# Four running tables in place of eight in a graph network's scatter, zeros written at the start, and a new order of two attention loops

## The chip, the cores and the metric

The kernel runs on one core of one Trainium2 chip. The metric is device time in microseconds (us), lower is better. Before the change three runs gave a median of 5661.89 us (5657.54 to 5664.57).

## What is computed

A graph with 3125 nodes of 128 features (padded to 3200, that is 25 blocks of 128) and 103125 edges, sorted by destination, goes through four layers: a GCN, an additive attention with 4 heads, a GAT with 2 heads, and an interaction layer. Each adds its result to `x`. The change touches the last one most. Cut to that, the reference is:

```python
xa = ssp(x)                          # softplus(x) - log 2
g = rbf @ k2f_W                      # one filter row per edge, from 64 attributes
msg = g * (xa @ Wj + bj)[idx_j]      # idx_j is the edge's destination
xj = segment_sum(msg, idx_i, n)      # idx_i is its source: in no order
m = xa @ Wi + bi + xj                # then residual blocks and a dense layer
```

The attention layers (additive and GAT) do for each edge: gather the source's projected row, add the destination's, apply tanh or leaky ReLU, multiply by an attention vector to a score, take a softmax over the edges of a destination, and sum the weighted source rows by destination.

## The kernel before, in words

Edges are cut into 202 tiles of 512 (`TILE`), four chunks of 128 (`SUB`). The kernel is a row of stages. A stage opens a block in which each engine has a program of its own, held together by semaphores; at its end all engines meet at a barrier (class `Stage`). SP issues the plain DMAs, POOL the indirect ones.

**`over_tiles`** (line 73) writes out the software pipeline of one engine: in step s it calls each function of its list, in the order of the list, for tile s minus that function's lag. The order of the list is thus the order in which an in-order engine does its work in a step. The change edits three such lists in `attend` (line 1321):
- on PE, for GAT, line 1461: scores (1412, 1415), turn_sums (1457), features (1399, 1403), sums (1443), turn (1424), turn_top (1434);
- on ACT, for the additive layer, line 1501: raise_scores (exp, line 1482), activate (tanh, 1476), keep_sums (1494);
- on DVE, for GAT, line 1552: tops (1521 to 1528), keep_sums (1548), onehots (1158), leaky (1514), edge_weights (1535), best_of_nodes (1541, 1544).

In both layers POOL gathers 128 rows for each chunk (line 744); a tile's gathers wait until the sums of the tile six before are done.

**`count_degrees`** (line 769), near the start, counts destinations: DVE makes one-hots (line 790) in 101 steps and PE multiplies them. SP has nothing to do until the counts are inverted; then it stores them (842) and loads them back (845, 847).

**The interaction.** `load_sources` (line 2079) loads the edges' sources, and clears eight tables in DRAM of 3200 + 128 rows of 128 float32: DVE makes 3200 zeros in each partition (2091), SP stores them eight times (2102), and 128 spare rows eight times (2104). The stage ends when all stores have landed. Then `scatter_filtered` (line 1162) makes 512 messages for each tile on PE, ACT and DVE: DVE compares the sources of a chunk with each other (1268), masks what lies above the diagonal (1273), so that a row that occurs twice in a chunk is summed by PE (1235) and goes out once, and the other is sent to a spare row (1295). ACT copies the rows out (1251). Last, POOL sends each chunk with an indirect DMA that adds into a table in DRAM (1309). Such a DMA reads its rows, adds, and writes them back, so two of them on the same table must not be under way at once. Table `sums[i][j]` is that of the tiles of parity i and chunk j, and so a chunk's scatter waits for that of the tile two before:

```python
for j in range(SUB):
    wait_count(pool, scattered[t.two][j], half_rounds(t) * 16)
pool.sem_inc(begun, 1)
for j in range(SUB):
    pool.indirect_dma_start(out=k.sums[t.two][j], ...)
```

ACT (1250) and DVE (1294) wait for the scatters of the tile four before, whose buffers they write over. `collect_sums` (line 2109) loads the eight tables one after another in three buffers (2122), and DVE copies the first (2132) and adds the other seven (2134).

Of the kernel before, what the change touches and what calls it, by code (L numbers as in the profile page):

```python
# [33 lines left out]
P = 128  # L34
# [134 lines left out]
def load_everything(k):  # L169
# [95 lines left out]

    k.sums = [[nc.dram_tensor(f"sums{i}_{j}", [N + P, F], F32).ap() for j in range(SUB)] for i in range(2)]
    k.all_counts = nc.dram_tensor("counts", [T, P, k.cells], FP16).ap()
# [501 lines left out]
def count_degrees(k):  # L769
# [23 lines left out]
    with Stage(k, "deg") as st:  # L793
        step, digits, high_ready, low_ready, counted = (st.sem("step"), st.sem("digits"), st.sem("high_ready"),
                                                        st.sem("low_ready"), st.sem("counted"))
        rooted, inverted, stored, spread = st.sem("rooted"), st.sem("inverted"), st.sem("stored"), st.sem("spread")
        with st.block() as block:
            @block.vector
            def _(dve):
# [39 lines left out]
            @block.sync  # L839
            def _(sp):  # L840
                sp.wait_ge(inverted, 1)
                sp.dma_start(k.isd.rearrange("(h l) -> h l", l=DIGIT), found).then_inc(stored, 16)
                sp.wait_ge(stored, 16)
                with nc.allow_non_contiguous_dma(reason="one number per node"):
                    sp.dma_start(k.inv_sqrt_deg[:, :], k.isd.rearrange("(o n) -> o n", o=1).to_broadcast(
                        [P, k.n_nodes])).then_inc(spread, 16)
                    sp.dma_start(k.inv_sqrt_deg_nm[:, :], k.isd.rearrange("(b p) -> p b", p=P)).then_inc(spread, 16)
                sp.wait_ge(spread, 32)


# [311 lines left out]
def scatter_filtered(k, table):  # L1162
# [8 lines left out]
    def one_pass():  # L1171
        with Stage(k, "filt") as st:
# [19 lines left out]
            with st.block() as block:  # L1192
# [107 lines left out]
                @block.gpsimd  # L1300
                def _(pool):
                    def scatter(t):
                        pool.wait_ge(out_ready, t.t + 1)
                        pool.wait_ge(row_ready, t.t + 1)
                        for j in range(SUB):
                            wait_count(pool, scattered[t.two][j], half_rounds(t) * 16)
                        pool.sem_inc(begun, 1)
                        for j in range(SUB):
                            pool.indirect_dma_start(  # L1309
                                out=k.sums[t.two][j], out_offset=bass.IndirectOffsetOnAxis(  # L1310
                                    ap=k.idx[t.slot][:, j:j + 1], axis=0),
                                in_=out_rows(t)[:, j, :], in_offset=None,
                                compute_op=ALU.add).then_inc(scattered[t.two][j], 16)
                    over_tiles(pool, k.tiles, [(1, scatter)])
                    for two in range(2):
                        for j in range(SUB):
                            pool.wait_ge(scattered[two][j], 16 * ceil_div(k.tiles - two, 2))
# [3 lines left out]
def attend(k, name, a, table, table_dst):  # L1321
# [33 lines left out]
    with Stage(k, name) as st:  # L1355
# [12 lines left out]
        with st.block() as block:  # L1368
# [20 lines left out]
            def _(pe):  # L1389
# [70 lines left out]
                if gat:  # L1460
                    over_tiles(pe, k.tiles, [(3, scores), (5, turn_sums), (1, features), (4, sums), (3, turn),
                                             (3, turn_top)], head=2, ring=DEEP)
                else:
# [4 lines left out]
            def _(act):  # L1468
# [31 lines left out]
                else:  # L1500
                    over_tiles(act, k.tiles, [(2, raise_scores), (1, activate), (4, keep_sums)], head=2, ring=DEEP)

            @block.vector
            def _(dve):
# [46 lines left out]
                if gat:  # L1551
                    over_tiles(dve, k.tiles, [(3, tops), (5, keep_sums), (0, onehots), (1, leaky),
                                              (3, edge_weights), (3, best_of_nodes)], head=2, ring=DEEP)
                else:
                    over_tiles(dve, k.tiles, [(0, onehots), (2, tops), (3, edge_weights)], head=2, ring=DEEP)
# [523 lines left out]
def load_sources(k):  # L2079
# [4 lines left out]
    k.earlier = k.fb[:, 0:SUB * P].rearrange("p (j e) -> p j e", e=P)  # L2084
    zeros = k.wide[:, 0, :]
    with Stage(k, "srcs") as st:
        loaded, cleared, zeroed = st.sem("loaded"), st.sem("cleared"), st.sem("zeroed")
        with st.block() as block:
            @block.vector
            def _(dve):  # L2090
                dve.memset(zeros, 0.0).then_inc(cleared, 1)
                dve.tensor_scalar(k.spare[:, :], k.iota_p[:, :], float(k.n_nodes), None, ALU.add)
# [4 lines left out]
            def _(sp):  # L2097
                sp.dma_start(raw, k.ins["src_edges"]).then_inc(loaded, 16)
                sp.wait_ge(cleared, 1)
                for two in k.sums:  # L2100
                    for table in two:
                        sp.dma_start(table[0:k.n_nodes, :].rearrange("(b p) f -> p b f", p=P),
                                     zeros.rearrange("p (b f) -> p b f", f=F)).then_inc(zeroed, 16)
                        sp.dma_start(table[k.n_nodes:k.n_nodes + P, :], zeros[:, 0:F]).then_inc(zeroed, 16)
                sp.wait_ge(loaded, 16)
                sp.wait_ge(zeroed, 32 * 2 * SUB)


def collect_sums(k):

    tables = [table for two in k.sums for table in two]
    total = k.h
# [133 lines left out]
```

## Time and profile before

| | us |
|---|---|
| median of three runs | 5661.89 |
| the profiled execution, its own time | 5659.49 |
| its span in the trace | 5657.8 |
| degree count, about | 45 to 176 |
| additive attention's loop | 910 to 1950 |
| GAT's loop | 2215 to 3530 |
| zeros and sources | 3768 to 3822 |
| scatter loop | 3841 to 5402 |
| collecting the tables | 5405 to 5461 |

Over the span PE is busy 70%, DVE 49%, POOL 55%, ACT 25%; but each stage has a limit of its own, so the stages are read one by one. "Busy" leaves out what an engine's sequencer does by itself: semaphores, register arithmetic, branches, and SP's issuing of DMAs. POOL's indirect DMAs count as busy while POOL makes their descriptors. The name in "idle before <- x" is what ended an engine's wait; "issue" means that nothing in the profile was waited for. PE's lines come twice, as PE (matmul) and PEld (loading of weights), which overlap. A letter q behind an engine means its sequencer.

### The profile page before, as it was taken

How to read it: one execution, taken by the hardware profiler on the slowest of the kernel's cores; microseconds unless marked ns; L12 is line 12 of the kernel's file. 1: busy time of each engine (PE TensorE's matmuls, PEld its weight loads, DVE VectorE, ACT ScalarE, POOL GpSimd, SP SyncE). 2: the span in 40 equal slices, each digit the busy share in tenths (PEclk: the TensorE clock that was granted, in tenths of full speed). 3: DMA queues.
4: the chain of work that ended last, by engine and by line, in shares of the span. 5: the costliest groups of instructions: out<-in, count | busy, mean ns of one | idle time of the engine just before them, and what ended most of it. 6: DMA issues, size and time to landing. Idle time of an engine off the chain costs nothing. (4 is left out here: it accounts for less than half of the span.)

```text
span 5657.8 us, 85234 instructions
## 1 busy us (share of the span) xinstructions
PE 3980.4 (70%) x18200; PEld 2339.9 (41%) x18200; DVE 2796.4 (49%) x7514; ACT 1440.7 (25%) x3414; POOL 3127.6 (55%) x3371
## 2 busy tenths in 40 slices
PE   3499564989888724999999999326666566656525
PEld 2233333555545412444444444015555555545401
DVE  7799123333333354555555555544444444444447
ACT  0233102333333212333333333011111111111125
POOL 0061123777777522555555554406888888888810
PEclk9999786887888756999999999565555555555557
DMA  1122332222222103333333332045566666666540
GB/s 31 34 67 88 97 96 69 69 70 69 69 69 69 41 0 97 99 97 97 98 97 97 97 97 75 1 114 100 94 96 97 95 97 96 97 96 96 88 100 12
DMA packets 515411, 447.78 MB, mean 79 GB/s; under 512 B 175623, under 2 KB 430678, under 8 KB 515030
## 3 DMA queue, kind: packets, MB, share of 16 engines
q0 software_dynamic: 180992, 211.97, 20.7%
q1 hardware_dynamic: 334294, 234.52, 15.2%
q14 instruction: 92, 0.75, 0.0%
q8 instruction: 33, 0.54, 0.0%
HBM read 336.65 MB, written 109.55 MB: 79 GB/s over the span
## 5 line engine op out<-in xcount | busy, mean ns | idle before, releaser
L1309 POOL DMA_INDIRECT sums<-gathered,idx x808 | 1307.3, 1618 | 419.0 <-issue 228.3
L744 POOL DMA_INDIRECT gathered<-table,idx x1088 | 1028.8, 946 | 796.8 <-DMA idx<-in_src_rows 285.2
L1415 PE MATMUL bank<-zact,att_cells 128*64 128x512 f32 (+1 forms) x1212 | 683.4, 676 | 0.9 <-ACT zact L1476 0.5
L744 POOL DMA_INDIRECT wide<-table,idx x528 | 498.8, 945 | 250.9 <-issue 135.7
L1235 PE MATMUL bank<-msg,gathered 128*128 128x128 f32 x1616 | 418.9, 441 | 262.6 <-DVE msg L1277 262.6
L1521 DVE TENSOR_REDUCE neg_raw<-bank 80x1 f32<-80x512 f32 (+1 forms) x404 | 276.5, 684 | 608.0 <-PE bank L1415 608.0
L1482 ACT ACTIVATE msg<-bank,neg_top 80x512 f32<-80x512 f32 (+1 forms) x404 | 275.9, 683 | 1121.2 <-DVE neg_top L1523 1116.2
L978 POOL TENSOR_TENSOR acc<-acc,msg 128x20 f32 x404 | 176.4, 437 | 617.9 <-issue 397.0
L1235 PEld LDWEIGHTS bank<-msg,gathered 128*128 128x128 f32 x1616 | 360.0, 328 | 315.7 <-DVE msg L1277 161.5
L1295 DVE TENSOR_TENSOR idx<-picked,partial 128x4 int32<-128x4 f32 x202 | 33.2, 164 | 803.3 <-DMA sums<-gathered,idx 802.3
L1217 PE MATMUL bank<-w_L_gnn_k2f_W,edge_rows 64*128 64x128 f32 x1616 | 418.9, 438 | 10.2 <-DMA edge_rows<-in_attr_rows 10.2
L1251 ACT COPY gathered<-bank 128x512 f32<-128x512 f32 x202 | 118.4, 586 | 1108.7 <-DMA sums<-gathered,idx 1101.4
L1217 PEld LDWEIGHTS bank<-w_L_gnn_k2f_W,edge_rows 64*128 64x128 f32 x1616 | 359.6, 325 | 55.6 <-issue 44.7
L1399 PE MATMUL bank<-ident,gathered 128*128 128x128 f32 x1632 | 292.1, 304 | 100.2 <-DMA gathered<-table,idx 98.8
L1225 PE MATMUL bank<-window,onehot_t 60*128 60x128 bf16 x808 | 121.3, 303 | 325.0 <-DVE onehot_t L1158 321.0
L1535 DVE COPY edge_rows<-bank 128x320 f32<-128x320 f32 (+1 forms) x404 | 185.2, 458 | 324.1 <-PE bank L1424 323.9
L1514 DVE TENSOR_TENSOR zact<-zact,bank 128x512 f32<-128x512 f32 x404 | 259.7, 684 | 149.4 <-ACT zact L1474 149.4
L1399 PEld LDWEIGHTS bank<-ident,gathered 128*128 128x128 f32 x1632 | 208.8, 152 | 266.4 <-issue 135.4
L927 DVE TENSOR_SCALAR gathered<-iota_c,partial 128x500 f16<-128x500 f16 x812 | 304.7, 391 | 3.3 <-issue 1.6
L1158 DVE TENSOR_SCALAR onehot_t<-dst_row,iota_w,always 64x512 bf16<-64x512 bf16 x606 | 264.5, 436 | 67.0 <-DMA dst_row<-local_rows 41.8
L1443 PE MATMUL bank<-gathered,edge_rows 128*64 128x256 f32 x1088 | 263.9, 385 | 0.0
L935 PE MATMUL bank<-gathered,zact 128*128 128x500 f16 x812 | 209.7, 381 | 69.9 <-DVE zact L928 59.4
(313 smaller groups left out, 6492.3 us busy)
## 6 DMA issues: line engine op xcount, KB each, us to landing
zact<-in_src_flat SPq DMA_DIRECT2D x202, 256.0 KB, 3.4
dst_row<-local_rows SPq DMA_DIRECT2D x606, 64.0 KB, 2.8
edge_rows<-in_attr_rows SPq DMA_DIRECT2D x202, 128.0 KB
gathered<-table,idx POOLq DMA_INDIRECT x1088, 2.7
sums<-gathered,idx POOLq DMA_INDIRECT x808, 3.5
sums<-wide SPq DMA_DIRECT2D x8, 1600.0 KB
counts<-wide SPq DMA_DIRECT2D x4, 3000.0 KB, 12.1
counts<-fm_ab SPq DMA_DIRECT2D x4, 3000.0 KB, 12.0
```

What stands on the lines that cost most here:

```text
L744: pool.indirect_dma_start(out=g[:, j, :], out_offset=None, in_=table, in_offset=bass.IndirectOffsetOnAxis(ap=k.idx[t.slot][:, j:j + 1], ax ...
L927: dve.tensor_scalar(k.cell_hot[slot][:, j, :], k.iota_c[:, :], k.cell[:, q], None, ALU.is_equal)
L1158: return dve.tensor_scalar(k.onehot_t[buf][:, :], k.dst_row[t.slot][:, :], k.iota_w[0:HROWS, 0:1], k.always[0:HROWS, 0:1], ALU.is_equal, A ...
L1217: mm = pe.matmul(k.bank[t.two][:, j * F:(j + 1) * F], k.attr[t.two][0:depth, j * P:(j + 1) * P], k.w["L3_gnn_k2f_W"][:, :], start=True, st ...
L1235: mm = pe.matmul(k.bank[4 + t.two][:, j * F:(j + 1) * F], same(t)[:, j, :], k.msg[t.two][:, j, :], start=True, stop=True)
L1309: pool.indirect_dma_start(out=k.sums[t.two][j], out_offset=bass.IndirectOffsetOnAxis(ap=k.idx[t.slot][:, j:j + 1], axis=0), in_=out_rows(t ...
L1399: pe.matmul(z_bank(t, h)[:, j * P:(j + 1) * P], g[:, j, h * F:(h + 1) * F], k.ident[:, :], is_transpose=True, start=(j == 0), stop=False, ...
L1415: mm = pe.matmul(score_bank(t), a.att[h][:, :], k.zact[t.two][:, h, :], start=False, stop=(h == a.zs - 1))
L1443: mm = pe.matmul(sum_bank(t), weights(t)[:, j, :], g[:, j, :], start=(j == 0), stop=(j == SUB - 1))
L1482: act.activation(raised(t), score_bank(t), ACT.Exp, bias=k.neg_top[0:cells, bass.ds(t.t, 1)], accum_out=k.weight_sum[0:cells, bass.ds(t.t, ...
L1514: m = dve.tensor_tensor(za, za, z_bank(t, h)[:, :], ALU.max)
L1521: dve.tensor_reduce(raw, score_bank(t), AX.X, ALU.max, negate=True).then_inc(top_found, 1)
```

## The change

- `load_sources` no longer clears tables. The clearing moves to `count_degrees`: POOL makes the zeros in `k.fa`, and SP stores them in four tables before it waits for the inverted counts. The stage waits for the stores at its end.
- Table `sums[j]` serves the chunk j of all tiles. A chunk's scatter waits for that of the same chunk of the tile before; wait and counter increment now stand ahead of each chunk's DMA.
- `collect_sums` reads four tables.
- PE's and DVE's order in GAT's loop and ACT's order in the additive loop change; the lags don't.

```diff
-    k.sums = [[nc.dram_tensor(f"sums{i}_{j}", [N + P, F], F32).ap() for j in range(SUB)] for i in range(2)]
+    k.sums = [nc.dram_tensor(f"sums{j}", [N + P, F], F32).ap() for j in range(SUB)]
...
+        cleared, zeroed = st.sem("cleared"), st.sem("zeroed")
         with st.block() as block:
+            @block.gpsimd
+            def _(pool):
+                pool.memset(k.fa[:, :], 0.0).then_inc(cleared, 1)
...
             @block.sync
             def _(sp):
+                sp.wait_ge(cleared, 1)
+                for table in k.sums:
+                    sp.dma_start(table[0:k.n_nodes, :].rearrange("(b p) f -> p b f", p=P),
+                                 k.fa[:, :].rearrange("p (b f) -> p b f", f=F)).then_inc(zeroed, 16)
+                    sp.dma_start(table[k.n_nodes:k.n_nodes + P, :], k.fa[:, 0:F]).then_inc(zeroed, 16)
                 sp.wait_ge(inverted, 1)
...
                 sp.wait_ge(spread, 32)
+                sp.wait_ge(zeroed, 32 * SUB)
...
                         for j in range(SUB):
-                            wait_count(pool, scattered[t.two][j], half_rounds(t) * 16)
-                        pool.sem_inc(begun, 1)
-                        for j in range(SUB):
+                            wait_count(pool, scattered[1 - t.two][j], (half_rounds(t) + t.two) * 16)
+                            pool.sem_inc(begun, 1)
                             pool.indirect_dma_start(
-                                out=k.sums[t.two][j], out_offset=bass.IndirectOffsetOnAxis(
+                                out=k.sums[j], out_offset=bass.IndirectOffsetOnAxis(
...
-                    over_tiles(pe, k.tiles, [(3, scores), (5, turn_sums), (1, features), (4, sums), (3, turn),
-                                             (3, turn_top)], head=2, ring=DEEP)
+                    over_tiles(pe, k.tiles, [(3, scores), (1, features), (5, turn_sums), (4, sums), (3, turn_top),
+                                             (3, turn)], head=2, ring=DEEP)
...
-                    over_tiles(act, k.tiles, [(2, raise_scores), (1, activate), (4, keep_sums)], head=2, ring=DEEP)
+                    over_tiles(act, k.tiles, [(1, activate), (2, raise_scores), (4, keep_sums)], head=2, ring=DEEP)
...
-                    over_tiles(dve, k.tiles, [(3, tops), (5, keep_sums), (0, onehots), (1, leaky),
-                                              (3, edge_weights), (3, best_of_nodes)], head=2, ring=DEEP)
+                    over_tiles(dve, k.tiles, [(3, tops), (0, onehots), (5, keep_sums), (1, leaky),
+                                              (3, best_of_nodes), (3, edge_weights)], head=2, ring=DEEP)
...
-    zeros = k.wide[:, 0, :]
...
-                dve.memset(zeros, 0.0).then_inc(cleared, 1)
...
-                sp.wait_ge(cleared, 1)
-                for two in k.sums:
-                    for table in two:
-                        sp.dma_start(table[0:k.n_nodes, :].rearrange("(b p) f -> p b f", p=P),
-                                     zeros.rearrange("p (b f) -> p b f", f=F)).then_inc(zeroed, 16)
-                        sp.dma_start(table[k.n_nodes:k.n_nodes + P, :], zeros[:, 0:F]).then_inc(zeroed, 16)
                 sp.wait_ge(loaded, 16)
-                sp.wait_ge(zeroed, 32 * 2 * SUB)
...
-    tables = [table for two in k.sums for table in two]
+    tables = k.sums
```

## Rows read from the trace of the kernel before

**Rows 1.** Windows by stage: busy us of each engine, clock, DMA share, GB/s

```profile
core 0: us, PE busy (x) PEld busy (x) DVE busy (x) ACT busy (x) POOL busy (x), PEclk, DMA share, GB/s
...
910.00:1950.00 1040.00, 909.56 (x4041) 518.28 (x4041) 345.06 (x812) 400.27 (x1419) 763.88 (x808) 0.81 0.28 67
2215.00:3530.00 1315.00, 1300.09 (x6261) 637.55 (x6260) 712.53 (x2019) 440.40 (x1017) 763.70 (x808) 0.99 0.34 96
3760.00:3841.00 81.00, 4.23 (x19) 3.45 (x19) 8.34 (x14) 2.64 (x9) 0.00 (x0) 0.50 0.71 206
3841.00:5402.00 1561.00, 940.17 (x4028) 786.62 (x4028) 689.84 (x1613) 236.26 (x403) 1307.30 (x808) 0.50 0.60 95
```

**Rows 2.** Timeline of the stage that clears the tables: start, us, what

```profile
3768.22 0.36 SPq L2098 DMA_DIRECT2D partial<-in_src_edges  x1
...
3771.62 0.57 DVE L2094 CAST partial<-partial 128x808 f32<-128x808 int32 x1
3771.72 0.37 SPq L2102 DMA_DIRECT2D sums<-wide  x1
...
3813.24 4.72 SPq L2104 DMA_DIRECT2D sums<-wide  x1
3822.08 0.06 DVE L517 MEMSET win_off<- 128x1 f32 x1 [49.89 <-PEq L158]
3822.93 0.33 DVE L429 TENSOR_SCALAR base<-first,win_off 128x202 f32<-128x202 f32 x1 [0.78 <-PEq L158]
```

**Rows 3.** Line 2134, adds of the collected tables, first and last start

```profile
L2134 DVE TENSOR_TENSOR h_nm<-h_nm,wide x5: 3492/3493/3493, 5423.4 to 5457.2; 128x3200 f32<-128x3200 f32 x5
```

**Rows 4.** Degree count: SP's first store, DVE's first steps; POOL's memsets by line

```profile
L842 SPq DMA_DIRECT2D isd<-h_nm x1: 342/342/342, 165.4 to 165.4; - x1
...
50.46 0.58 DVE L801 TENSOR_SCALAR wide<-dst_f 128x808 f32<-128x808 f32 x1 [0.70 <-PEq L158]
...
L322 POOL MEMSET ident<- x1: 195/195/195, 1.5 to 1.5; 128x128 f32 x1
...
L327 POOL MEMSET head_row<- x1: 301/301/301, 2.0 to 2.0; 2x256 f32 x1
```

**Rows 5.** Line 1309, the scatters: duration ns, waits before them, time to landing

```profile
L1309 POOL DMA_INDIRECT sums<-gathered,idx x808: 1558/1558/2300, 3847.3 to 5399.1; - x162
...
  issue: 228.3, 749
...
  DMA sums<-gathered,idx: 16.5, 54
...
DMA to landing us min/median/max: 3.2/3.5/5.2
```

**Rows 6.** Timeline, ACT's last work ahead of the first scatter, and that scatter

```profile
3845.81 0.59 ACT L1251 COPY gathered<-bank 128x512 f32<-128x512 f32 x1 [1.42 <-PE bank L1235]
...
3847.30 2.12 POOL L1309 DMA_INDIRECT sums<-gathered,idx  x1 [172.94 <-ACT gathered L1251]
```

**Rows 7.** Line 1307, the increment on POOL's sequencer

```profile
L1307 POOLq EVENT_SEMAPHORE  x202: 42/43/43, 3846.4 to 5387.6; - x101
```

**Rows 8.** Timeline of the scatter loop: DVE's mask and the POOL scatter beside it

```profile
4606.50 0.69 DVE L1273 TENSOR_TENSOR fm_ab<-gathered,lower 128x512 f32<-128x512 f32 x1
...
4607.22 1.56 POOL L1309 DMA_INDIRECT sums<-gathered,idx  x1 [0.30 <-issue]
...
4622.41 0.69 DVE L1273 TENSOR_TENSOR fm_ab<-gathered,lower 128x512 f32<-128x512 f32 x1
4622.47 2.06 POOL L1309 DMA_INDIRECT sums<-gathered,idx  x1 [0.30 <-issue]
```

**Rows 9.** Timeline of one step of GAT's loop, PE and DVE

```profile
2704.66 0.40 PE L1412 MATMUL bank<-onehot_t,far 64*64 64x512 bf16 x1
...
2705.69 0.17 DVE L1544 TENSOR_TENSOR fm_ab<-fm_ab,bank 2x20 f32 x1
...
2706.85 0.33 PE L1457 MATMUL bank<-ident,tile_rows 64*128 64x64 f32 x2
...
2709.41 1.28 DVE L1514 TENSOR_TENSOR zact<-zact,bank 128x512 f32<-128x512 f32 x2 [0.72 <-ACT zact L1474]
...
2711.06 0.40 PE L1412 MATMUL bank<-onehot_t,far 64*64 64x512 bf16 x1
```

**Rows 10.** Waits in the additive loop, 1000 to 1900, POOL's longest

```profile
POOL gathered L744 <- issue: 131.0, 430, 0.3
```

More of the change, by code:

```diff
@@ L2084, in load_sources @@
     k.earlier = k.fb[:, 0:SUB * P].rearrange("p (j e) -> p j e", e=P)
-    zeros = k.wide[:, 0, :]
     with Stage(k, "srcs") as st:
-        loaded, cleared, zeroed = st.sem("loaded"), st.sem("cleared"), st.sem("zeroed")
+        loaded = st.sem("loaded")
         with st.block() as block:
```

## The prediction

> **What bounds the kernel now.** I read the windows by stage first, because the shares of the whole page mix stages with different limits; then, in each stage that the diff touches, the timeline of one step and the waits ahead of the busiest engine's instructions. Four limits come out.
>
> The additive loop belongs to POOL. Its 808 gathers are 763.88 us busy in 1040 [rows 1], 0.945 us each, and each has a gap of 0.30 us before it that waits for nothing (131.0 us in 430) [rows 10]. 808 x 1.25 = 1010 us, nearly all of the loop.
>
> GAT's loop belongs to PE: 1300.09 us busy in 1315, at a granted clock of 0.99, which is the 2.4 GHz level [rows 1]. One step lasts from one L1412 to the next, 2711.06 - 2704.66 = 6.40 us [rows 9].
>
> The stage that clears the tables belongs to the DMA engines: 206 GB/s in a window of which it fills two thirds, and no engine computes [rows 1]. Collecting belongs to them too: DVE's adds last 3.49 us but start every (5457.2 - 5423.4) / 6 = 5.63 us [rows 3].
>
> The scatter loop belongs to POOL again: 1307.30 us busy in 1561 [rows 1]. A scatter takes 1558 ns at the median and 1618 at the mean (1307.30 / 808), and the gap before it is 228.3 / 749 = 0.305 us [rows 5]. A tile is 4 x (1.618 + 0.305) = 7.69 us, 202 of them 1553 us. PE runs there at half clock, the 1.2 GHz level, and has 4.7 us of work in a tile: it is not the limit.
>
> **The zeros.** Before, the stage's first DMA goes out at 3768.22 and the next stage's first instruction starts at 3822.08 [rows 2]. What stays is the load of the sources and the cast behind it, which ends at 3771.62 + 0.57 = 3772.19; the memset that goes ran beside that load. A stage's barrier takes 0.78 us between the two DVE instructions at 3822.08 and 3822.93 [rows 2]; with a semaphore to clear I take 0.9. The next stage would start at 3773.1. **Gain 49.0 us**, sure to a microsecond.
>
> In the degree count four tables take half of what eight took. Eight took SP from 3771.72 to about 3818 [rows 2], so four take some 24 us. POOL's memset of 3200 columns comes first: 128 columns took 195 ns and 256 took 301 [rows 4], so 0.83 ns a column and 3200 columns about 2.75 us. The stage starts near 50.46, so SP is free again near 80, and is wanted at 165.4 [rows 4]: 80 us to spare, hidden behind DVE's one-hots. Without that cover it would cost the 24 us. Nothing else is in SP's queue in that stage. What the stage may lose is DVE time beside POOL's memset, since DVE's first steps read and write SBUF at the same moment. No row shows such a pair. Least is 0, most is the whole memset, 2.75; I take 1.5, **loss 1.5 us**. The Trainium skill (SBUF — State Buffer, Who interferes with whom) has DVE and GpSimd share a port pair as an exclusive lock for DVE's two-port modes; by that the loss would be near the upper end, and the sum 1 us less.
>
> **Collecting.** Four tables fewer at 5.63 us each: **gain 22.5 us**. The first load's latency stays, and so does the last add.
>
> **The scatters.** The wait moves from the tile two before to the tile before. A chunk's predecessor on its table was issued four scatters earlier, at least 4 x (1.558 + 0.305) = 7.45 us. It lands 3.5 us after its issue at the median and 5.2 at the latest [rows 5]. From a released wait to POOL's start there are 3847.30 - (3845.81 + 0.59) = 0.90 us [rows 6]. Latest case: 5.2 + 0.9 = 6.1 us, 1.3 less than 7.45. So the wait is always met, at the median with 3 us to spare. Queued behind it on POOL are only the later chunks, and ACT and DVE, which wait for the tile four before, are three tiles ahead. What is added on POOL's sequencer is three more increments a tile, 43 ns each [rows 7], and the register arithmetic of the waits. In the 54 cases where a landing was the last thing that POOL waited for, the gap was 16.5 / 54 = 0.306 us, as without it [rows 5]: sequencer work lies beside the descriptors of the scatter before. Bounds: 0 and 202 x 3 x 0.043 = 26 us. I take 0, since the gap does not see the sequencer.
>
> **GAT's order.** PE does the same eight groups in a step with as many changes of group, so as long as it never waits the step stays at 6.40. Checked in time from L1412: the transposes L1457 move from 2.2 to about 3.7 us, and their needs, the last of which is best_of_nodes of the step before, ending 1.2 us into this one (2705.69 + 0.17) [rows 9], are met earlier still in relation to them. DVE's keep_sums behind them ends near 4.35; leaky, now behind it on DVE, starts at 2709.41, that is 4.75 [rows 9], because it waits for ACT. So no new delay, with 0.4 us to spare. Edge weights come last on DVE, up to 0.9 us later, near 1.4 us into the next step, and are needed at 4.0. The bounds are what one change of group more or less would cost; I have about 0.1 us, so 202 x 0.1 = 20 us either way, and take 0. **The additive layer's** ACT order: tanh comes some 0.3 us sooner, exp later; POOL sets the pace there, so 0, within 2.
>
> **Sum.** -49.0 + 1.5 - 22.5 = -70.0 us. The profiled execution's own time is 5659.49, which gives 5589.5. The median is 2.4 higher: 5591.9, I say 5592 us. A measurement of this kernel can tell about 0.2% (11 us) from no change.
>
> **Rivals.** *A stall behind the new wait (slower).* If the landing that POOL sees, plus POOL's restart, exceeded 7.45 us, each tile would last as long as that round trip. It eats the gain of 70 us when a tile takes 7.69 + 70 / 202 = 8.04 us, a landing of 7.1 us. For it: two read-modify-writes of one table now follow closely, and nothing before did that. Against: the longest of 808 landings took 5.2 [rows 5]. At a round trip of 8.2 us: +0.51 x 202 = +103, so 5695 us. The Trainium skill (DMA: Bandwidth & Descriptors, Anatomy of one DMA) puts most of a DMA's fixed time in the receipt of the write, longest towards HBM; it speaks against waiting closely, and the landing rows already hold that time. 4%.
>
> *The sequencer shows.* The three increments or more lie open: +26, so 5618. 8%.
>
> *DVE's phase against POOL.* A scatter that started 0.06 us behind DVE's mask took 2.06 us, one that started just after the mask's end 1.56 [rows 8]. All excess over the median is (1618 - 1558) ns x 808 = 48 us [rows 5]. If the new waits shift the phase so that all such meetings go, the time is 5592 - 48 = 5544; if they double, 5640. The phase is set by landings, which I expect unchanged. 4% for less by over half of that, 5% for more. The Trainium skill (SBUF — State Buffer, Who interferes with whom) says that a tensor_tensor with two SBUF inputs blocks GpSimd's reads but, as it infers, not descriptor generation; by that the excess has another cause and would stay.
>
> *GAT's loop moves.* A change of group saved, or a wait of ACT or DVE off PE's path: 5572, 9%; one more, 5612, 6%.
>
> **How the numbers follow.** The forecast as it stands (within 12 us) has 64%. The range of 8 in 10 takes in both GAT cases and the open sequencer: 5568 to 5622. Outside stay the stall, and the phase at its ends. Faster by over 0.2% is all but the stall and some unforeseen loss: 0.94; the same 0.02; slower 0.04.
>
> **What would show it.** After: L517 near 3774.6 with no SP stores before it; SP's stores to the tables between 53 and 85, and the store L842 within 3 us of 165.4; three adds in L2134 at 5.6 us; L1309 with a mean of 1.60 to 1.64 us and gaps of 0.305; steps of 6.40 in GAT. Wrong, if POOL's line has waits over 0.31 us that a landing ended, if L1309's mean leaves that band, or if PE shows idle time before any group of GAT's loop.

## The result: 103 us faster, 33 more than forecast

The changed kernel takes 5560.19 us (median of 4 runs, 5553.14 to 5562.94); the kernel before took 5663.23 beside it (4 runs). The ratio is 0.9817, with a 95% interval from 0.98 to 0.9834. The forecast was 5592 with a range from 5568 to 5622, so the sign was right and the size was not. The profiled execution has a span of 5551.4 us, 106.4 less than before.

The length of each stage in the two traces, from barrier to barrier (for the zeros, from the stage's first DMA to the next stage's first instruction):

| stage | before | after | difference | forecast |
|---|---|---|---|---|
| zeros and sources | 53.86 | 4.53 | -49.3 | -49.0 |
| degree count | 126.2 | 128.4 | +2.2 | +1.5 |
| collecting the tables | 52.4 | 29.9 | -22.5 | -22.5 |
| GAT's loop | 1318.0 | 1288.6 | **-29.4** | **0** |
| scatter loop | 1576.5 | 1571.3 | -5.2 | 0 |
| additive loop | 1033.9 | 1031.0 | -2.9 | 0 |

They make -107.1; all other stages together come to +0.7.

In the changed kernel's line numbers, GAT's groups on PE are: far 1422 and scores 1425 (together the stage function scores), features 1409 and 1413, turn_sums 1467, sums 1453, turn_top 1444, turn 1434.

### The profile page after: what moved, and what is told of

Its sections match the earlier page's. It is cut to its first block and busy times, and to the rows that moved or that the text cites. A ratio compares the mean times of both kernels' runs of the same rounds, so it can differ in the third digit from the quotient of the medians.

```text
span 5551.4 us, 85617 instructions
## 1 busy us (share of the span) xinstructions
PE 3951.9 (71%) x18200; PEld 2354.3 (42%) x18200; DVE 2792.4 (50%) x7509; ACT 1416.9 (26%) x3414; POOL 3127.3 (56%) x3372
## 5 line engine op out<-in xcount | busy, mean ns | idle before, releaser
L1319 POOL DMA_INDIRECT sums<-gathered,idx x808 | 1302.4, 1612 | 369.0 <-issue 169.8
L938 DVE TENSOR_SCALAR gathered<-iota_c,partial 128x500 f16<-128x500 f16 x812 | 275.4, 339 | 3.8 <-issue 1.4
L1486 ACT ACTIVATE zact<-bank 128x512 f32<-128x512 f32 x202 | 120.7, 597 | 570.0 <-PE bank L1413 570.0
```

What stands on the lines that cost most here:

```text
L938: dve.tensor_scalar(k.cell_hot[slot][:, j, :], k.iota_c[:, :], k.cell[:, q], None, ALU.is_equal)
L1319: pool.indirect_dma_start(out=k.sums[j], out_offset=bass.IndirectOffsetOnAxis(ap=k.idx[t.slot][:, j:j + 1], axis=0), in_=out_rows(t)[:, j, ...
```

## The profile after

The windows of the changed kernel, against [rows 1]; columns: window and length, then busy time of PE, PEld, DVE, ACT, POOL, granted clock, DMA share, GB/s:

```profile
910.00:1950.00 1040.00, 908.65 (x4047) 516.15 (x4045) 344.20 (x820) 391.43 (x1425) 764.66 (x808) 0.81 0.27 67
2215.00:3530.00 1315.00, 1284.58 (x6281) 657.90 (x6280) 736.14 (x2072) 429.00 (x1020) 775.22 (x856) 0.98 0.35 96
```

PE is 1284.58 us busy in the window that held 1300.09 before, at almost the same clock (0.98 for 0.99, both the 2.4 GHz level). Nothing was taken out of PE's work: the same groups run, and the window now also holds some 20 us behind the loop's end. One step of the changed kernel, PE's rows of the timeline, against [rows 9]:

```profile
2700.93 0.40 PE L1422 MATMUL bank<-onehot_t,far 64*64 64x512 bf16 x1
2701.26 1.93 PE L1425 MATMUL bank<-zact,att_cells 128*64 128x512 f32 x4
2703.12 1.09 PE L1409 MATMUL bank<-ident,wide 128*128 128x128 f32 x8
2704.14 0.60 PE L1413 MATMUL bank<-onehot_t,window 60*128 60x512 bf16 x2
2704.59 0.28 PE L1467 MATMUL bank<-ident,tile_rows 64*128 64x64 f32 x2
2704.80 1.94 PE L1453 MATMUL bank<-gathered,edge_rows 128*64 128x256 f32 x8
2706.67 0.20 PE L1444 MATMUL bank<-top_cells,own 64*2 64x20 f32 x2
2706.80 0.46 PE L1434 MATMUL bank<-ident,msg 64*128 64x64 f32 x4
2707.19 0.40 PE L1422 MATMUL bank<-onehot_t,far 64*64 64x512 bf16 x1
```

and the same step of the kernel before, of which [rows 9] holds only three PE rows:

```profile
2704.99 1.93 PE L1415 MATMUL bank<-zact,att_cells 128*64 128x512 f32 x4
...
2707.11 1.09 PE L1399 MATMUL bank<-ident,gathered 128*128 128x128 f32 x8
2708.14 0.60 PE L1403 MATMUL bank<-onehot_t,window 60*128 60x512 bf16 x2
2708.67 1.94 PE L1443 MATMUL bank<-gathered,edge_rows 128*64 128x256 f32 x8
2710.54 0.46 PE L1424 MATMUL bank<-ident,msg 64*128 64x64 f32 x4
2710.93 0.20 PE L1434 MATMUL bank<-top_cells,own 64*2 64x20 f32 x2
```

None of these rows has an idle time in brackets: PE never waited, before or after. A step is 2707.19 - 2700.93 = 6.26 us where it was 6.40. Subtract neighbouring starts. Window features to the next group: 2708.67 - 2708.14 = 0.53 before, 2704.59 - 2704.14 = 0.45 after. From turn_sums to the next group: 2707.11 - 2706.85 = 0.26 before, 2704.80 - 2704.59 = 0.21 after. All else agrees to 0.01. These two make the 0.14 to 0.15 us of a step, and over 201 steps the loop's 29 us.

What is special about that pair is printed in the rows: behind PE's operand names stands the shape of the weights, rows times columns. The window features use 60*128, the turned sums 64*128; both fill 64 rows by 128 columns when rows are rounded up to 64 or 128. turn_top's 64*2 counts as a shape of its own: from its last matmul to the next group it is 0.106 to 0.107 us at the median, whether far (64*64), turn or, in a later run, the features follow, against 0.027 between its own two. Written so, a step before had eight changes of shape, the change has seven, because these two groups now stand side by side.

The weight loads show what a change does. The first load of turn_sums, before and after, and that of sums in the run g7_top_between, where sums stands right behind scores with the same shape:

```profile
2706.84 0.20 PEld L1457 LDWEIGHTS bank<-ident,tile_rows 64*128 64x128 f32 x2 [0.81 <-issue]
```

```profile
2704.37 0.35 PEld L1467 LDWEIGHTS bank<-ident,tile_rows 64*128 64x128 f32 x2
```

```profile
2702.92 0.14 PEld L1453 LDWEIGHTS bank<-wide,edge_rows 128*64 128x64 f32 x1 [0.29 <-issue]
```

With a change of shape the load starts only together with its own matmul (2706.84 for 2706.85); with equal shapes it starts beside the matmul before, 0.22 us ahead of its own (2704.37 for 2704.59) and 0.42 ahead in the third (2702.92 for 2703.34). At all eight kinds of change in the trace before, the median start of the load lies within 0.02 us of its own matmul's. So a change takes away the overlap of the next load with the matmul before it.

The scatter loop, line 1319, against [rows 5] (durations ns, waits before them, time to landing):

```profile
L1319 POOL DMA_INDIRECT sums<-gathered,idx x808: 1558/1559/2282, 3768.1 to 5314.9; - x162
  issue: 169.8, 557
...
  DMA sums<-gathered,idx: 75.0, 246
...
DMA to landing us min/median/max: 3.2/3.4/4.9
```

A landing is now named as the last thing waited for 246 times in place of 54, as it should be with a wait twice as near, and the mean gap is 75.0 / 246 = 0.305 us, exactly that of the gaps without. The wait is always met in time. The page's row for the line gives the mean duration:

```profile
L1319 POOL DMA_INDIRECT sums<-gathered,idx x808 | 1302.4, 1612 | 369.0 <-issue 169.8
```

1302.4 us for 1307.30 [rows 1]: the 4.9 us are nearly all that this loop gained. Scatters of over 1.6 us are 116 in place of 125. Of those 125, 121 started while a VectorE operation ran, 115 of them beside one of two: the comparison (line 1268) and the mask (line 1273), whose operands both lie in SBUF. These 115 lasted longer by what was left of that operation, less 0.127 us at the median (0.617 left, 0.490 longer); eight that started within 0.05 us of its start were not held. The 43 scatters that started beside line 1277, which takes as long and reads one operand from PSUM, were longer by 0.05 us all together, and the 49 beside the reduction (line 1282) by 0.04.

The degree count's start, timeline, against [rows 4]:

```profile
50.22 2.76 POOL L801 MEMSET fm_ab<- 128x3200 f32 x1 [42.39 <-POOLq L158]
...
50.26 3.15 DVE L806 TENSOR_SCALAR wide<-dst_f 128x808 f32<-128x808 f32 x1 [0.70 <-PEq L158]
53.01 0.39 SPq L848 DMA_DIRECT2D sums<-fm_ab  x1
...
53.45 0.58 DVE L809 TENSOR_SCALAR wide<-wide 128x808 f32<-128x808 f32 x1
```

VectorE's first operation takes 3.15 us where it took 0.58, and ends at 53.41, 0.43 after GpSimd's memset; the next one of the same size, with GpSimd idle, is back at 0.58.

Where the zeros were written, and the end of collecting, timelines of the two stages, against [rows 2, 3]:

```profile
3738.58 0.36 SPq L2106 DMA_DIRECT2D partial<-in_src_edges  x1
...
3741.80 0.58 DVE L2102 CAST partial<-partial 128x808 f32<-128x808 int32 x1 [3.03 <-DMA partial<-in_src_edges]
3743.11 0.06 DVE L517 MEMSET win_off<- 128x1 f32 x1 [0.73 <-PEq L158]
```

```profile
5339.33 3.49 DVE L2135 TENSOR_TENSOR h_nm<-h_nm,wide 128x3200 f32<-128x3200 f32 x1 [3.82 <-DMA wide<-sums]
5345.00 3.49 DVE L2135 TENSOR_TENSOR h_nm<-h_nm,acc 128x3200 f32<-128x3200 f32 x1 [2.18 <-DMA acc<-sums]
5350.51 3.49 DVE L2135 TENSOR_TENSOR h_nm<-h_nm,wide 128x3200 f32<-128x3200 f32 x1 [2.02 <-DMA wide<-sums]
```

No SP store is left before the next stage; three adds remain, 5.5 to 5.7 us apart.

## The experiments

The theory: **(A)** PE pays for each change of the rounded weight shape, about 0.146 us, also between two groups of which neither ever waits. Rivals: VectorE's new order, or the exchange of the two short groups, made the step shorter.

The runs were made in three sessions. In the first two the kernel before itself took 6019.89 us (4 runs) and 5963.54 us (20 runs), and the traces of the changed kernel and its variants have longer attention loops there; so the single step says more than the total. The expectations call a session a chip. The first ran on chip 8, the other two on chip 0, where the kernel before took 5963.54 us in one and 5657.96 in the other, so the number of the chip does not settle it. Steps are counted from one start of far to the next, 201 in a loop. A step counts for the commonest value when it is within 0.02 us of it.

### One engine's order at a time

**g2_dve_old**: PE's new order, VectorE's old one.

```diff
-                    over_tiles(dve, k.tiles, [(3, tops), (0, onehots), (5, keep_sums), (1, leaky),
-                                              (3, best_of_nodes), (3, edge_weights)], head=2, ring=DEEP)
+                    over_tiles(dve, k.tiles, [(3, tops), (5, keep_sums), (0, onehots), (1, leaky),
+                                              (3, edge_weights), (3, best_of_nodes)], head=2, ring=DEEP)
```

> The changed kernel with DVE's old order in GAT's loop; PE's new order stays. Theory A: PE pays about 0.146 us whenever the array shape of its weights changes (rows rounded up to 64 or 128, columns to 32, 64 or 128), and the new order has 7 such changes in a step in place of 8. Then DVE's order is nothing: steps of 6.26 us, about 5560 us in all. Theory B: the gain of 0.146 us a step comes from DVE, which does best_of_nodes earlier and so releases the transposes of line 1467 earlier. Then steps of 6.41 us, about 5590 us. Theory C: the swap of turn and turn_top did it. As A for this run.

**g3_pe_old**: PE's old order, VectorE's new one.

```diff
-                    over_tiles(pe, k.tiles, [(3, scores), (1, features), (5, turn_sums), (4, sums), (3, turn_top),
-                                             (3, turn)], head=2, ring=DEEP)
+                    over_tiles(pe, k.tiles, [(3, scores), (5, turn_sums), (1, features), (4, sums), (3, turn),
+                                             (3, turn_top)], head=2, ring=DEEP)
```

> The changed kernel with PE's old order in GAT's loop; DVE's new order stays. Theory A (changes of array shape): 8 changes again, steps of 6.41 us, +29 us, about 5590 us. Theory B (DVE releases PE earlier): steps of 6.26 us, about 5560 us. Theory C (swap of turn and turn_top): 6.41 us.

**g4_swap_only**: VectorE's order old, and PE's old but for the last two:

```diff
-[(3, scores), (1, features), (5, turn_sums), (4, sums), (3, turn_top), (3, turn)]
+[(3, scores), (5, turn_sums), (1, features), (4, sums), (3, turn_top), (3, turn)]
```

> The changed kernel with both old orders in GAT's loop, but for the swap of turn and turn_top on PE, which stays. Theory A: still 8 changes of array shape, steps of 6.41 us, about 5590 us. Theory B: 6.41 us. Theory C: the swap is what saves, steps of 6.26 us, about 5560 us.

Measured (kernel before 6019.89 us):

| | us | ratio (interval) | commonest step | start of scores' last matmul to next group |
|---|---|---|---|---|
| g2_dve_old | 5990.6 | 0.9949 (0.9913 to 0.9985) | 6.26 (149) | 0.523 |
| g3_pe_old | 5955.88 | 0.9889 (0.9861 to 0.9918) | 6.41 (62) | 0.523 at least, 0.78 median |
| g4_swap_only | 5963.2 | 0.9901 (0.9873 to 0.993) | 6.41 (18) | 0.523 at least, 0.87 median |

The step follows PE's order and not VectorE's, and the exchange alone does not shorten it: but for the loop's last, no step of g4 is shorter than 6.40 us, and one of g3 (6.38). In g4 only 18 steps are free of stalls, so there the evidence is thin. The totals don't follow the step, and the expected 5560 and 5590 us were met by none: g2 has the shorter step and is the slowest of the three. Its GAT loop takes 1435.5 us against 1415.7 and 1408.5, because in that first session a part of the steps is disturbed; in g2 44 of 201 last over 6.5 us. In g3 and g4 the transposes right behind the scores also wait in most steps. So these three settle where the saving of an undisturbed step comes from, by the step alone, and no more.

### Moving turn_sums beside turn

**g5_together**: features, then sums, then the three short groups.

```diff
-[(3, scores), (1, features), (5, turn_sums), (4, sums), (3, turn_top), (3, turn)]
+[(3, scores), (1, features), (4, sums), (5, turn_sums), (3, turn), (3, turn_top)]
```

> The changed kernel with turn_sums moved once more on PE: scores, features, sums, turn_sums, turn, turn_top. It no longer follows the matmul of line 1413, but it now stands ahead of turn, whose transposes have the same array shape (64 rows, 128 columns). Theory A: 7 changes, as after the change, though at another place: steps of 6.26 us, about 5560 us. Rival D: what saves is that fp32 weights are loaded early behind a bf16 matmul, or that turn_sums stands behind features; then 6.41 us, about 5590 us. A stall on DVE's keep_sums, now late, would show as PE idle time and more than 6.41.

It took 5953.84 us, ratio 0.9886 (0.9857 to 0.9915). PE's rows of its timeline:

```profile
2967.64 0.34 PE L1467 MATMUL bank<-ident,tile_rows 64*128 64x64 f32 x2
2967.82 0.41 PE L1434 MATMUL bank<-ident,msg 64*128 64x64 f32 x4
2968.59 0.20 PE L1444 MATMUL bank<-top_cells,own 64*2 64x20 f32 x2 [0.35 <-DVE partial L1558]
2968.74 0.38 PE L1422 MATMUL bank<-onehot_t,far 64*64 64x512 bf16 x1
```

Between turn_sums and turn, two groups of the same shape, no charge is seen: turn's first matmul starts 0.062 us behind turn_sums's last, as turn's own matmuls do behind each other. But turn_top shares a PSUM bank with the turned sums and waits until VectorE has copied them: 0.35 us of idle, and a commonest step of 6.67, where theory A expected 6.26. From turn's last start to turn_top's first it is 0.554 at the median, 0.40 more than without the wait; take that off and 6.27 is left, as A has it for seven changes. But the whole step was not shorter, so this says nothing yet of a gain.

### The changed kernel again, and an order with five changes

**a1_after_again** is the changed kernel, unedited.

> The changed kernel once more, as it is, beside the three others of this group: its ratio to the kernel before is the mark for them. On the first chip it was 0.982 with GAT's steps at 6.26 us in place of 6.41. On a chip like that of the first four experiments, where the kernel before takes 6020 us, I expect 0.982 to 0.99.

It took 5924.1 us (5917.17 to 5941.46), ratio 0.9938 (0.9918 to 0.9958): 39 us less than the kernel before in that session, where the same pair was 103 apart. The windows of the additive loop, the changed kernel's first profile and then this one's:

```profile
915.00:1946.00 1031.00, 906.99 (x4040) 515.26 (x4040) 342.53 (x808) 389.27 (x1414) 764.66 (x808) 0.81 0.28 68
```

```profile
916.00:2188.00 1272.00, 965.50 (x4040) 565.17 (x4040) 334.71 (x808) 381.00 (x1414) 765.20 (x808) 0.70 0.22 55
```

The same instructions, POOL busy to within 0.6 us, and 241 us more in which it is idle; GAT's loop takes 1408.7 us for 1288.6, though its commonest step is still 6.26 (140 of 201). Scatter loop, zeros, degree count and collecting are unchanged within 1.2 us. The zeros and the collecting alone gave 70 us in the first pair, so with 39 in all something else, most likely the attention loops, cost the changed kernel some 30 us more than the kernel before in that session, shorter step or not. There is no trace of the kernel before from that session to tell; why the loops lose time there stays open.

**g6_five_changes**: scores and sums (both 128 by 64) adjacent, and window features, turn_sums and turn (all 64 by 128) adjacent.

```diff
-[(3, scores), (1, features), (5, turn_sums), (4, sums), (3, turn_top), (3, turn)]
+[(4, turn_top), (3, scores), (4, sums), (1, features), (5, turn_sums), (3, turn)]
...
-over_tiles(act, k.tiles, [(3, raise_scores), (1, activate), (4, copy_sums)], head=2, ring=DEEP)
+over_tiles(act, k.tiles, [(3, raise_scores), (4, copy_sums), (1, activate)], head=2, ring=DEEP)
...
-[(3, tops), (0, onehots), (5, keep_sums), (1, leaky), (3, best_of_nodes), (3, edge_weights)]
+[(4, best_of_nodes), (3, tops), (0, onehots), (5, keep_sums), (3, edge_weights), (1, leaky)]
```

> The changed kernel with GAT's loop in an order made for theory A (each change of array shape costs PE 0.146 us): PE turn_top of the tile four before, scores, sums, features, turn_sums, turn, which has 5 changes of shape in a step in place of 7 (8 before); ACT and DVE follow. Theory A: 6.26 - 2 x 0.146 = 5.97 us a step, -59 us against the changed kernel, about 1% less. Rival B or D (the gain came from what turn_sums waits for or stands behind): 6.26 us or more, and the whole not faster. A stall of DVE, which now has its leaky ReLU last, would show as PE idle time ahead of line 1422 or 1425.

It took 5974.06 us, ratio 1.0021 (1.0008 to 1.0034): 50 us more than a1, where 59 less were expected. A plain miss, and the wait in front of turn_top (line 1444, its matmuls and weight loads together) shows half of why:

```profile
  issue: 222.9, 227
  DVE partial L1558: 83.0, 170
```

The savings are there: from scores' last start to sums' first 0.429, the spacing inside scores, where features came at 0.523. But turn_top now stands two groups behind turn_sums and waits in most steps for VectorE's copy, so turn's last start to turn_top's first is 0.556 at the median and 0.152 at the least. 0.40 us are lost for 0.29 gained, and the commonest step is 6.38. That 0.12 us in 201 steps is half of the 50 us; the GAT loop as a whole is 52 us longer than a1's, and the rest of that lies in disturbed steps.

### The same five changes without the stall

**g7_top_between**: turn_top now between sums and features. It needs only what VectorE copied a whole step earlier; the number of changes stays five. ACT's order as in g6.

```diff
-[(4, turn_top), (3, scores), (4, sums), (1, features), (5, turn_sums), (3, turn)]
+[(3, scores), (4, sums), (4, turn_top), (1, features), (5, turn_sums), (3, turn)]
...
-[(4, best_of_nodes), (3, tops), (0, onehots), (5, keep_sums), (3, edge_weights), (1, leaky)]
+[(3, tops), (0, onehots), (4, best_of_nodes), (5, keep_sums), (3, edge_weights), (1, leaky)]
```

> GAT loop only. TensorE's order is (3, scores), (4, sums), (4, turn_top), (1, features), (5, turn_sums), (3, turn): the five changes of array shape of the order before this one, but turn_top now stands where it needs only what VectorE copied one step earlier, so that the 0.40 us stall before it should be gone. Theory A (each change of shape costs 0.146 us, whatever the groups compute): the common step falls from 6.26 to about 6.26 - 2 x 0.146 = 5.97 us, the loop by 201 x 0.29 = 58 us against the changed kernel, of which the part in undisturbed steps is seen in full; and the spacing from the last start of scores to the first of sums is 0.43, as inside scores. On a chip where the kernel before takes about 5960: about 5865, ratio near 0.984. Rival B (turn_sums's place alone gained the 0.146, changes of shape elsewhere are free): the step stays at 6.26 and the time at that of the changed kernel, ratio near 0.994. Rival C (another engine closes in once TensorE has 0.29 us less to do): the step ends above 6.0 with idle stretches of TensorE that end on VectorE or ScalarE.

It took **5498.86 us** (5 runs, 5495.19 to 5503.62) in a session in which the kernel before took 5657.96 (9 runs): ratio 0.9718 (0.9705 to 0.9731). That is 159 us less than the kernel before, where the changed kernel was 103 less: 56 us more, and 58 were expected. (The changed kernel was not run again beside it, so that comparison goes by way of the kernel before; the expected ratio of 0.984 was for a session like the second.) Its GAT loop takes 1232.9 us for 1288.6, and 198 of 201 steps last 5.98. One of them:

```profile
2701.25 0.40 PE L1422 MATMUL bank<-onehot_t,far 64*64 64x512 bf16 x1
2701.58 1.93 PE L1425 MATMUL bank<-zact,att_cells 128*64 128x512 f32 x4
2703.34 1.89 PE L1453 MATMUL bank<-wide,edge_rows 128*64 128x256 f32 x8
2705.16 0.20 PE L1444 MATMUL bank<-top_cells,own 64*2 64x20 f32 x2
2705.30 1.09 PE L1409 MATMUL bank<-ident,gathered 128*128 128x128 f32 x8
2706.32 0.60 PE L1413 MATMUL bank<-onehot_t,window 60*128 60x512 bf16 x2
2706.76 0.28 PE L1467 MATMUL bank<-ident,tile_rows 64*128 64x64 f32 x2
2706.88 0.41 PE L1434 MATMUL bank<-ident,msg 64*128 64x64 f32 x4
2707.22 0.40 PE L1422 MATMUL bank<-onehot_t,far 64*64 64x512 bf16 x1
```

Group by group, from each start to the next, us:

| group | before | after | g7 |
|---|---|---|---|
| far | 0.33 | 0.33 | 0.33 |
| scores | 1.86 | 1.86 | 1.76 |
| features, 128 rows | 1.03 | 1.02 | 1.02 |
| features, window | 0.53 | 0.45 | 0.44 |
| turn_sums | 0.26 | 0.21 | 0.12 |
| sums | 1.87 | 1.87 | 1.82 |
| turn | 0.39 | 0.39 | 0.34 |
| turn_top | 0.13 | 0.13 | 0.14 |
| changes of shape | 8 | 7 | 5 |
| step | 6.40 | 6.26 | 5.97 |

Each change taken away shortens two entries: the group before it by 0.08 to 0.10 us, the group behind it by about 0.05 (in turn_sums, behind a change, its second matmul starts 0.112 us after the first, without one 0.060). Three times equal shapes now stand side by side (window and turn_sums, scores and sums, turn_sums and turn), and 6.407 - 5.977 = 0.43 us with them, 0.143 each. PE is idle ahead of none of these rows, and the next busiest engine, POOL, works 696.03 us in 1100 of the loop. Rivals B and C fall, and so does rival D of g5_together: scores and sums are both float32, with no bf16 matmul between them, and their weights are loaded early too.

### The other suspects

**z1_zeros_late**: the tables are still four, but their zeros go back to the stage that loads the sources.

```diff
-                pool.memset(k.fa[:, :], 0.0).then_inc(cleared, 1)
...
+                dve.memset(zeros, 0.0).then_inc(cleared, 1)
...
+                for table in k.sums:
+                    sp.dma_start(table[0:k.n_nodes, :].rearrange("(b p) f -> p b f", p=P),
+                                 zeros.rearrange("p (b f) -> p b f", f=F)).then_inc(zeroed, 16)
```

> The changed kernel with the zeros of its four tables back in the stage that loads the sources, made by DVE. My sum: four tables take 24.5 us there, and the degree count gets 2.2 us back that DVE lost beside POOL's memset: +22 us against the changed kernel. Rival: the stores cost the degree count something else too, or the DMA engines' latency dominates in the late stage; then the difference is not 20 to 25 us.

5948.47 us, ratio 0.9977 (0.9965 to 0.999); 24 more than a1. 22 were expected. That stage takes 30.20 us in place of 4.53, the degree count 126.2 in place of 128.4: +25.7 and -2.2. So of the 47 us that the zeros gave, half (25.7 - 2.2 = 23.5) comes from writing them where SP has nothing to do, and half (53.86 - 30.20 = 23.7) from having four tables to clear and not eight.

**s1_two_tables**: a chunk's scatter waits for the one two before it, not four; the tables are two.

```diff
-    k.sums = [nc.dram_tensor(f"sums{j}", [N + P, F], F32).ap() for j in range(SUB)]
+    k.sums = [nc.dram_tensor(f"sums{j}", [N + P, F], F32).ap() for j in range(2)]
...
-                            wait_count(pool, scattered[1 - t.two][j], (half_rounds(t) + t.two) * 16)
+                            if j < 2:
+                                wait_count(pool, scattered[1 - t.two][j + 2], (half_rounds(t) + t.two) * 16)
+                            else:
+                                wait_count(pool, scattered[t.two][j - 2], (half_rounds(t) + 1) * 16)
...
-                                out=k.sums[j], out_offset=bass.IndirectOffsetOnAxis(
+                                out=k.sums[j % 2], out_offset=bass.IndirectOffsetOnAxis(
```

> The changed kernel with two tables in place of four: a chunk's scatter waits for the one issued two before it. Collecting saves 2 x 5.63 = 11 us. Theory: a scatter lands 3.5 us after its issue and POOL needs up to 0.9 us from a released wait to its next start, so two scatters take 4.4 us in place of 3.8 and a tile 8.9 us in place of 7.66: +250 us less 11, and POOL's waits carry idle times above 0.31 us. If POOL's restart costs only the 0.3 us that every gap has, two scatters take 3.8 to 3.9 us, and it is +10 to +30 us less 11. If the sequencer's extra work showed, both would be above this.

6203.35 us, ratio 1.0398 (1.0377 to 1.0419), 279 more than a1. The scatters' waits:

```profile
  DMA sums<-gathered,idx: 269.4, 207
  issue: 267.9, 600
```

Here a landing costs 269.4 / 207 = 1.30 us a time, and the gaps put down to "issue" have grown from 0.305 to 267.9 / 600 = 0.447 us, so they hold some of the wait too; both together, less 0.305 a scatter, are 291 us. By that much the scatter loop is longer (1863.1 us for a1's 1572.4), where the theory expected 250, and collecting takes 11 less. One of the round trips in its timeline:

```profile
4701.09 1.56 POOL L1322 DMA_INDIRECT sums<-gathered,idx  x1 [0.30 <-issue]
...
4703.22 1.56 POOL L1322 DMA_INDIRECT sums<-gathered,idx  x1 [0.58 <-issue]
...
4705.87 1.56 POOL L1322 DMA_INDIRECT sums<-gathered,idx  x1 [1.10 <-DMA sums<-gathered,idx]
```

From a scatter's start to that of the one which waits for it: 4705.87 - 4701.09 = 4.78 us. Over all such pairs of this loop the median is 4.5 and the longest 6.4. Two scatters with their gaps need only 3.73, four need 7.45. So the round trip fits in four scatters, with 3 us to spare at the median and 1 at the worst, and not in two: the rival with a stall behind the new wait is real, one halving further on.

**b2_top_between_early**: g7, and the zeros come from an array that GpSimd clears in the setup stage.

```diff
+                pool.memset(k.fb[:, :], 0.0)
                 pool.memset(k.best[:, :], 0.0).then_inc(flat, 1)
...
-                pool.memset(k.fa[:, :], 0.0).then_inc(cleared, 1)
```

> The same order of the GAT loop, and the zeros for the four tables come from an array that GpSimd clears in the setup stage, ahead of the degree count, in place of one that it clears beside the degree count's first operations. If those 2.76 us of GpSimd beside VectorE's 3.15 us (0.58 before) are what the degree count's stage lost, that stage comes back by about 2.2 us and the setup stage, where GpSimd has other memsets while the inputs load, grows by less than that. Against the kernel with the new order alone: minus 2 us at best, which the timing can hardly show and the stage lengths can. If the setup stage is set by GpSimd, it grows by up to 2.8 us and nothing is won.

5500.56 us, ratio 0.9722 (0.9709 to 0.9736), not to be told from g7. The stages show what the total can't: the degree count takes 125.8 us for 128.4, the setup 37.1 for 36.9. Its timeline of the degree count's start:

```profile
50.31 0.39 SPq L844 DMA_DIRECT2D sums<-fm_ab  x1
50.35 0.58 DVE L803 TENSOR_SCALAR wide<-dst_f 128x808 f32<-128x808 f32 x1 [0.70 <-PEq L158]
```

VectorE's first operation is back at 0.58 us beside SP's stores; so it was GpSimd's memset that held it, and not the DMA.

## Why the prediction was right and wrong

**The zeros: right** (-49.3 for -49.0; L517 starts 0.73 us after the cast's end, at 3743.11 and not near 3774.6, because the loops ahead of it are shorter by some 31 us). In the degree count the stores L842 (now 852) start at 167.8 for 165.4, within the 3 us named. The charge for the memset was 2.2, where I took 1.5 between 0 and 2.75. The operation beside it grew by 3.15 - 0.58 = 2.57 us, so the upper end was nearer, which is where the Trainium skill (SBUF — State Buffer, Who interferes with whom) put it, and this trace agrees with its lock: VectorE's operation, which started 0.04 us after the memset, ended 0.43 us after the memset's end.

**Collecting: right**, -22.5.

**The scatters: right in the mechanism.** The wait is never seen: gaps of 0.305 us, a longest landing of 4.9 us, and the mean 1.612 us in the band of 1.60 to 1.64. The trace tells the landing of 505 scatters of 808 only, and before of 404, so the prediction's "longest of 808 landings" was the longest of 404; the gaps, which are whole, carry the argument without them. s1 shows that the wait is seen at half the distance. Three more increments on POOL's sequencer cost nothing visible. What is left, 5 us in fewer slow scatters, was the rival of the phase, a tenth of its size. That rival's last sentence does not hold here: the excess has no other cause than the VectorE operation. Of the 48.4 us of excess in the trace before, 44.2 lie in scatters that started beside lines 1268 and 1273, by the rule of what was left of them.

**GAT's order: wrong, and this is the step that failed:** "PE does the same eight groups in a step with as many changes of group, so as long as it never waits the step stays at 6.40." PE does not wait, before or after, but a change of group is not what costs. A change of array shape costs, 0.143 to 0.147 us, and the new order has one less of those. Both were in the rows I had looked at: the shapes are printed in them, and window features to the next group took 0.53 us where two matmuls of 512 columns need 0.45 (0.227 from one to the other). The bound for one such change, "about 0.1 us", was too small as well: it gave 20 us, and 29 were measured. And the case in which it happens was taken as a rival at 9%, when counting shapes would have made it the forecast: -70.0 - 29.4 = -99.4, that is 5562 to 5563 by the forecast's own steps, within 3 us of what was measured. The Trainium skill (TensorEngine Tiling (Array Packing), Tiling Modes) says that changing the tiling mode drains the TensorE. It gives no price; these traces agree with it, since no load of a new shape starts beside the matmul before, and they put 0.14 us on each change, in ordinary matmuls too.

**The additive loop: nearly**, -2.9 for 0 within 2. The same loop took 1033.0 us in g7's trace, 0.9 less than before, so 2 of the 2.9 us are what two traces of the same code differ by. POOL is busy in it for 764.66 us in place of 763.88.

**Chance and range.** The range ended at 5568, 8 us above the result. It took in the rival with the bound of 0.1 us, which had no row behind it where a change of shape measured 0.14, and left 5 and 3 us of small gains in two other loops without a place.

## What to carry to other kernels

Where PE is the bound and never waits, write the weight shape of each group beside its name and order the groups so that equal shapes are neighbours. In these traces 60 and 64 rows counted as equal, and rows or columns alone were enough for a change (64*64 to 128*64, 64*128 to 64*64); where else the borders lie no run shows. In this loop each change saved is worth 0.14 us a step, if the group that moves still finds its inputs ready. Look for who shares a PSUM bank with it: g6 and g7 have the same number of changes, and one group's place makes 0.40 us a step between them. A wait may be moved nearer as long as the round trip (here 4.5 us at the median and 6.4 at the most for a scatter, restart included) stays below what the issuing engine does in between.

## What the hardware showed that was not expected

- A change of PE's array shape costs 0.14 us at the 2.4 GHz level with no wait: 0.08 to 0.10 ahead of the first matmul of the new shape, about 0.05 behind it. The weight load of the new shape does not start beside the matmul before.
- A VectorE operation on float32 in SBUF that started 0.04 us after a GpSimd memset was held until 0.43 us after the memset's end (3.15 us beside 2.76, 0.58 alone).
- An indirect scatter that started beside a VectorE operation with two operands in SBUF took 1.56 us plus what was left of that operation, less 0.13; an operation with one operand in PSUM, or a reduction, did not hold it.
- The same kernel can take 5924 us in one session and 5560 in another, with nearly all of the difference in two loops. Its undisturbed steps are alike to 0.01 us, so steps carry over where totals don't. What disturbs the rest was not found.
